# Scattering rows by source: an index bound on the indirect DMAs, or real places for the padding rows

## The chip, the cores and the metric

The kernel runs on one core of one Trainium2 chip. The metric is the device time of one execution in microseconds (us); less is better. Three timed executions of the kernel before gave 6073.62, 6076.83 and 6087.9 us.

## What is computed

A graph of N = 6250 nodes with 128 features and E = 106250 edges (50000 drawn pairs in both directions, and a loop for each node), sorted by destination, goes through four layers, each followed by a layer norm of the sum with its input:

```python
x = _layernorm(x + _L0_gnn_ref(...))   # attention over the edges into each node, 8 heads
x = _layernorm(x + _L1_gnn_ref(...))   # an MLP per edge, summed by destination
x = _layernorm(x + _L2_gnn_ref(...))   # a filter per edge times a projected row, summed by destination
x = _layernorm(x + _L3_gnn_ref(...))   # gated layer
```

The change concerns how the last layer gets its second mean. In `_L3_gnn_ref` both directions of each edge are used:

```python
a_in  = _seg_mean(feat_in[src], dst, N)    # mean over the edges into a node
a_out = _seg_mean(feat_out[dst], src, N)   # mean over the edges out of a node
h = _gru_cell(jnp.concatenate((a_in, a_out), axis=1), h, ...)
```

The first mean follows the order in which the edges lie. The second needs them by source, and they are sorted by destination.

## The kernel before, in words

**Tiles.** Nodes lie in buckets of P = 128 (NB = 49). The edges, sorted by destination, are cut into tiles of 128 so that no tile spans two buckets; a bucket's last tile is padded. There are TILES = 880 tiles, 4 (U) to a batch, 220 (BATCHES) batches, and R = 4 ring slots of one batch each. 880 x 128 = 112640 places stand for 106250 edges, so 6390 rows are padding.

**Stages.** The program is a row of stages in order of time, each with its own loops on all engines and with a barrier behind it: a short set-up, attention (126 to 1345 us of the span), the edge MLP (1451 to 2566), the filter layer (2610 to 3718, and its end), the scatter of rows by source (3738 to 4897) and the gated layer (4907 to 6026, and its end). In four of these GpSimd (POOL) gathers one row for each edge with `gather_rows`: one indirect DMA per tile, four per batch, with no bound on the index. In the fifth it scatters.

**The scatter.** The class `RowsBySource` takes one batch k at a time. SP loads the tile's local destination numbers (`load`, L762), VectorE makes a one-hot of them (`one_hot`, L2081), TensorE multiplies it with the node rows (`rows_of`, L2089), ScalarE puts 128 features, a one and the local source number into a row of REV = 130 words, 520 bytes (`pack`, L2096 and L2098), and POOL sends each tile's 128 rows to their places in the table `by_src` in device memory (`scatter`, L2105). `pack` waits until the scatters that used the same ring slot four batches earlier have landed. The first EARLY = 12 batches are done in the filter layer's block, the other 208 in `stage_rows_by_src`, whose POOL loop ends with a wait for all landings (L2117 is the end of that block).

**The places.** The table has RB = 256 blocks of 512 rows (SLOTS_R = 131072), filled in layer 1 with rows that count for nothing. The place of each row is an integer in `key_i`. It is worked out in the filter layer by VectorE in 16 steps of `number(n)` (L1678 to L1715), one per batch from batch R = 4 on, each on 128x880 values; `numbered` counts them. In step 7 the padding rows get a place beyond the table (`wrong`, 4 x SLOTS), step 11 makes the integers, steps 12 to 15 make the local source numbers. A padding row's index is beyond SLOTS_R - 1, and the bound makes the DMA leave that row out:

```python
pool.indirect_dma_start(self.table, bass.IndirectOffsetOnAxis(place, 0), self.out[:, r, u, :], None,
                        bounds_check=SLOTS_R - 1, oob_is_err=False).then_inc(self.scattered[r], 16)
```

Three engines wait for `numbered` to reach 16 before they start on the early batches: SP ahead of its first twelve `load`s, ScalarE ahead of the first `pack`, VectorE ahead of the memset of the ones (L1874). The gated layer reads the 256 blocks of the table in order (L2252).

Of the kernel before, what the change touches and what calls it, by code (L numbers as in the profile page):

```python
# [21 lines left out]
ALU = mybir.AluOpType  # L22
# [7 lines left out]
P = 128  # L30
# [8 lines left out]
U = 4  # L39
R = 4  # L40
KR, FR = 6, 7
TILES = -(-(E // P + NB) // (U * R)) * U * R
# [3 lines left out]
RB = (E + NB * QUAD) // QUAD  # L46
SLOTS_R = RB * QUAD
# [3 lines left out]
REV = F + 2  # L51
# [95 lines left out]
def arena(c, start, shape, dtype=F32):  # L147
    n = 1
    for s in shape:
        n *= s  # L150
    words = n if dtype != BF16 else n // 2
    ap = c.arena[:, start:start + words]
    if dtype != F32:
        ap = ap.bitcast(dtype)
    if len(shape) == 2:
        return ap.rearrange("p (a b) -> p a b", b=shape[1])
    if len(shape) == 3:
        return ap.rearrange("p (a b c) -> p a b c", b=shape[1], c=shape[2])
    return ap
# [537 lines left out]
def is_first(k):  # L697
    return isinstance(k, int) and k == 0
# [9 lines left out]
def bucket_in_turn(nc, c, n, engine):  # L708

    return nc.values_load_multi_w_load_instructions(  # L710
        c.order[:, n:n + 1], engines=(engine,), min_val=0, max_val=NB - 1,
        skip_runtime_bounds_check_because="the vector engine made them within these bounds")[1][0]
# [586 lines left out]
def stage_edges(nc, c, name, table, acc, buckets, local, layer, h1, next_rows=None):  # L1299
# [5 lines left out]
    with ExitStack() as ctx:  # L1305
# [34 lines left out]
        if layer == 2:  # L1340
            by_tile = arena(c, SPOTS0, [JC, P])
            slot, high7, high9, wrong = (arena(c, RANKS0 + n * TILES, [TILES]) for n in range(4))
            row = arena(c, NUMBERS0, [TILES])
            whole, shifted = (arena(c, NUMBERS0 + n * TILES, [TILES], I32) for n in range(1, 3))
            pslot, spotted, numbered = pb("pslot", [P, 2, 512]), sem("spotted"), sem("numbered")
# [32 lines left out]
        @block.sync  # L1378
        def _(sp):
            def send_row(k):  # L1380
                n = BUCKET_AT.get(k)
                if n is None:
                    return
                at = bucket_in_turn(nc, c, n, SP_ENGINE)
                sp.wait_ge(kept, n + 1)
                sp.dma_start(next_rows[bass.ds(at, 1), :, :].rearrange("one p f -> p (one f)"), keep[:, n % 3, :]).then_inc(row_sent[n % 3], 16)

            def step(k, i, r):
                if layer == 1 and k >= 17:
                    send_row(k - 17)  # L1390
                if k >= BATCHES:
                    return
                e0 = loaded_values(nc, c.edge0, k, SP_ENGINE, E - 1)

                at_least(sp, ready, k - R + 1, tick)
                if layer == 1:
                    at_least(sp, hots_t, k - R + 1, tick)
                    load_local_rows(sp, c, rows, k, r, rows_in)
                for u in range(U):
                    to = attr[u * A1:(u + 1) * A1, r, :] if layer == 1 else attr[:, r, u * P:(u + 1) * P]  # L1400
                    sp.dma_start(to, attr_dram[:, bass.ds(e0[u], P)]).then_inc(attributes[r], 16)
                if layer == 1:
                    if k == R * NB + 8:
                        sp.wait_ge(ranked, 3 + 6 * NB)
                        sp.dma_start(c.slots.rearrange("(p n) -> p n", p=P), slot_of).then_inc(slotted, 16)
                    if is_first(k):
                        sp.wait_ge(start, 3)
                        sp.dma_start(next_rows[NT - 1:NT, :, :].rearrange("one p f -> p (one f)"), filler[:, 0, 0:F]).then_inc(filled, 16)
                    for b in range(k, RB, BATCHES):
                        sp.dma_start(c.by_src[bass.ds(b, 1), :, :, :].rearrange("one p u f -> p (one u) f"), filler[:, :, :]).then_inc(filled, 16)  # L1410
            if layer == 1:
                sp.dma_start(src_i, c.src.rearrange("(p n) -> p n", p=P)).then_inc(sources, 16)
            rounds(sp, BATCHES, R, step)
            if layer == 2:
                sp.wait_ge(numbered, 16)
                for k in range(EARLY):
                    c.by_source.load(sp, k)
            if layer == 1:
                for k in range(BATCHES, BATCHES + 17):
                    step(k, k // R, k % R)  # L1420
                sp.wait_ge(slotted, 16)
                sp.wait_ge(filled, 16 * (RB + 1))
                for n in range(3):
                    sp.wait_ge(row_sent[n], 16 * len(range(n, NB, 3)))

        @block.scalar
        def _(act):
# [91 lines left out]
            def pack_early(k, i, r):  # L1519
                b = k + 14 - BATCHES - EARLY_LAG  # L1520
                if 0 <= b < EARLY:
                    if b == 0:
                        act.wait_ge(numbered, 16)
                        act.wait_ge(c.by_source.start, 1)
                    c.by_source.pack(act, b, pt)

# [125 lines left out]
        def _(dve):  # L1652
# [25 lines left out]
            def number(n):  # L1678
                if n == 0:
                    dve.wait_ge(spotted, 1)  # L1680
                if n:
                    dve.wait_ge(numbered, n)
                if n == 0:
                    ins = dve.tensor_copy(slot[:, 0:512], pslot[:, 0, :])
                if n == 1:
                    ins = dve.tensor_copy(slot[:, 512:TILES], pslot[:, 1, 0:TILES - 512])
                if n == 2:
                    ins = dve.tensor_copy(whole, slot)
                if n == 3:
                    ins = dve.tensor_scalar(shifted, whole, 7, None, ALU.arith_shift_right)  # L1690
                if n == 4:
                    ins = dve.tensor_copy(high7, shifted)
                if n == 5:
                    ins = dve.tensor_scalar(shifted, whole, 9, None, ALU.arith_shift_right)
                if n == 6:
                    ins = dve.tensor_copy(high9, shifted)
                if n == 7:
                    ins = dve.tensor_scalar(wrong, c.key[:, :], 0.0, float(4 * SLOTS), ALU.is_lt, ALU.mult)
                if n == 8:
                    ins = dve.scalar_tensor_tensor(out=row, in0=slot, scalar=4.0, in1=wrong, op0=ALU.mult, op1=ALU.add)  # L1700
                if n == 9:
                    ins = dve.scalar_tensor_tensor(out=row, in0=high7, scalar=-511.0, in1=row, op0=ALU.mult, op1=ALU.add)
                if n == 10:
                    ins = dve.scalar_tensor_tensor(out=row, in0=high9, scalar=508.0, in1=row, op0=ALU.mult, op1=ALU.add)
                if n == 11:
                    ins = dve.tensor_copy(c.key_i, row)
                if n == 12:
                    ins = dve.tensor_scalar(shifted, c.gather_i[:, :], 7, None, ALU.arith_shift_right)
                if n == 13:
                    ins = dve.tensor_copy(high7, shifted)  # L1710
                if n == 14:
                    ins = dve.tensor_copy(high9, c.gather_i[:, :])
                if n == 15:
                    ins = dve.scalar_tensor_tensor(out=c.src_local[:, :], in0=high7, scalar=-float(P), in1=high9, op0=ALU.mult, op1=ALU.add)
                ins.then_inc(numbered, 1)  # L1715

# [124 lines left out]
            def step(k, i, r):  # L1841
# [20 lines left out]
                    cut_off(k - CUT_AT)  # L1862
                if layer == 1 and CUT_AT + 8 <= k < CUT_AT + 10:
                    cut_off(k - CUT_AT - 4)
                if layer == 2 and R <= k < R + 16:
                    number(k - R)
                for lag, part in node_steps:
                    if k - lag in BUCKET_AT:
# [1 line left out]
                b = k - BATCHES - EARLY_LAG  # L1870
                if layer == 2 and 0 <= b < EARLY:
                    if b == 0:
                        dve.wait_ge(numbered, 16)
                        dve.memset(c.by_source.out[:, :, :, F:F + 1], 1.0).then_inc(c.by_source.start, 1)  # L1874
                    c.by_source.one_hot(dve, b)
            rounds(dve, BATCHES, R, step, peeled=2)
            for k in range(BATCHES, BATCHES + 17):
                step(k, k // R, k % R)
# [181 lines left out]
class RowsBySource:  # L2060
# [39 lines left out]
    def scatter(self, pool, k):  # L2100
        r = k % R
        pool.wait_ge(self.packed, 2 * (k + 1))
        for u in range(U):
            place = self.c.key_i[:, k * U + u:k * U + u + 1]
            pool.indirect_dma_start(self.table, bass.IndirectOffsetOnAxis(place, 0), self.out[:, r, u, :], None,  # L2105
                                    bounds_check=SLOTS_R - 1, oob_is_err=False).then_inc(self.scattered[r], 16)

EARLY, EARLY_LAG = 12, 2
# [374 lines left out]
def gnn_kernel(nc, t, out):  # L2484
    c = Core(nc)
    scratch = lambda name, shape: nc.dram_tensor(name, shape, F32, kind="Internal").ap()
    c.by_src = scratch("rows_by_src", (RB, P, U, REV))
    c.slots = scratch("slots", (EP,))
    c.kv3 = scratch("keys_values", (NT, P, 2 * F))
    c.kv = c.kv3.rearrange("t p f -> (t p) f")  # L2490
# [83 lines left out]
```

## Time and profile before

| what | value |
|---|---|
| timed runs, median (lowest to highest) | 6076.83 us (6073.62 to 6087.9) |
| the profiled execution's own time | 6069.62 us |
| its span, first to last instruction | 6067.6 us |
| busy: POOL, TensorE, VectorE, ScalarE | 4297.3, 3856.3, 3649.1, 2834.3 us |
| five sweeps of 880 indirect DMAs on POOL | 838.8 to 869.3 us busy each |
| granted TensorE clock, mean | 0.776 |

The profiled execution's time and its span are 2.0 us apart; what is worked out from its rows is set against its own 6069.62 us. Busy times are sums over the whole span. An engine whose busy share is high in every stage is a candidate for the bound of each; whether it is shows in who waits for whom inside a stage. "Issue" in a list of waits is idle time in which the profile sees nothing that the engine waited for.

### The profile page before, as it was taken

The numbers are of one execution on the slowest core, as the hardware profiler recorded it, in microseconds if no ns is written. First come the engines' busy times: TensorE is split into PE (matmuls) and PEld (weight loads), VectorE is DVE, ScalarE is ACT, GpSimd is POOL, SyncE is SP. The second block draws the span as 40 slices with busy tenths as digits, with TensorE's granted clock in tenths as the row PEclk, the third lists the DMA queues.
The fourth block names the chain that finished last, engine by engine and source line by source line (L and its number), as shares of the span: only waits on it lengthen the run. The fifth ranks groups of instructions, "written<-read, shape, count | busy, mean of one in ns | idle before, by whom it ended". The sixth has DMA issues, their size and how long they took to land. (4 is left out here: it accounts for less than half of the span.)

```text
span 6067.6 us, 93535 instructions
## 1 busy us (share of the span) xinstructions
PE 3856.3 (64%) x20652; PEld 3144.4 (52%) x20652; DVE 3649.1 (60%) x11761; ACT 2834.3 (47%) x6936; POOL 4297.3 (71%) x4477
## 2 busy tenths in 40 slices
PE   5567767765666767678888876344343446666665
PEld 4566666664555555546556554333333346665443
DVE  6788888886988888667777774111001034445665
ACT  3788888882111111355555563111111158884444
POOL 2677777663777777767777776677777777777775
PEclk8787787787999898878888887555555579898777
DMA  4444444453655555622223324332222245553223
GB/s 125 123 134 129 128 129 128 123 117 103 189 148 147 147 148 148 126 64 74 74 74 74 74 74 62 100 77 77 77 75 75 73 115 168 163 164 89 59 59 46
DMA packets 485366, 649.31 MB, mean 107 GB/s; under 512 B 120187, under 2 KB 332938, under 8 KB 484822
## 3 DMA queue, kind: packets, MB, share of 16 engines
q0 software_dynamic: 155552, 345.75, 22.9%
q1 hardware_dynamic: 329271, 297.58, 18.2%
q8 instruction: 187, 3.06, 0.2%
q14 instruction: 356, 2.92, 0.2%
HBM read 495.44 MB, written 150.71 MB: 106 GB/s over the span
## 5 line engine op out<-in xcount | busy, mean ns | idle before, releaser
L694 POOL DMA_INDIRECT kv_ring<-keys_values,gather_i x880 | 860.8, 978 | 363.9 <-issue 247.9
L2105 POOL DMA_INDIRECT rows_by_src<-arena,key x880 | 869.3, 988 | 309.7 <-issue 260.2
L694 POOL DMA_INDIRECT e_ring<-filter_rows,gather_i x880 | 838.8, 953 | 304.8 <-issue 268.0
L694 POOL DMA_INDIRECT e_ring<-table,gather_i x880 | 845.7, 961 | 287.2 <-issue 264.6
L694 POOL DMA_INDIRECT arena<-table,gather_i x880 | 850.6, 967 | 278.8 <-issue 266.7
L2089 PE MATMUL rs_ph<-nodes,arena 128*128 x1664 | 424.4, 436 | 667.7 <-ACT arena L2098 615.6
L2089 PEld LDWEIGHTS rs_ph<-nodes,arena 128*128 128x128 f32 x1664 | 365.5, 324 | 726.9 <-issue 726.9
L2081 DVE TENSOR_SCALAR arena<-arena,part 128x512 f32<-128x512 bf16 x220 | 113.6, 519 | 949.2 <-PE rs_ph L2089 898.3
L1565 PE MATMUL e_pa<-e_msg,e_hot 128*128 128x128 f32 x3520 | 552.5, 308 | 37.0 <-DVE e_msg L1768 30.2
L743 DVE TENSOR_TENSOR arena<-arena,e_pa 128x128 f32 x1760 | 496.9, 282 | 110.8 <-PE e_pa L1565 81.9
L2331 PE MATMUL gl_sum_f<-arena,gl_hot_f 128*128 128x128 f32 x1760 | 292.8, 318 | 425.3 <-DMA arena<-table,gather_i 198.5
L1565 PEld LDWEIGHTS e_pa<-e_msg,e_hot 128*128 128x128 f32 x3520 | 511.5, 223 | 49.2 <-DVE e_msg L1768 41.9
L930 PE MATMUL at_pa<-at_msg,at_hot 128*128 128x145 f32 x1760 | 356.7, 359 | 235.0 <-DVE at_msg L1200 148.6
L2096 ACT ACTIVATE arena<-src_local 128x4 f32<-128x4 bf16 x220 | 45.8, 208 | 972.5 <-DMA rows_by_src<-arena,key 934.5
L2331 PEld LDWEIGHTS gl_sum_f<-arena,gl_hot_f 128*128 128x128 f32 x1760 | 253.1, 221 | 463.7 <-issue 242.8
L1546 PE MATMUL e_ph<-l_w1e_by_tile,e_attr 128*128 128x512 f32 x440 | 274.4, 709 | 334.0 <-DVE e_tmp L1763 313.3
L930 PEld LDWEIGHTS at_pa<-at_msg,at_hot 128*128 128x128 f32 x1760 | 300.2, 239 | 278.7 <-DVE at_msg L1200 214.8
L1445 ACT ACTIVATE e_msg<-e_tmp 128x512 f32<-128x512 f32 x220 | 138.6, 630 | 634.4 <-DVE e_tmp L1763 625.8
L1537 PE MATMUL e_pt<-e_attr,L_mlp_w_held 50*128 50x512 f32 x440 | 279.2, 718 | 172.0 <-DVE e_soft L1774 169.1
L2278 ACT ACTIVATE gl_hot_r<-j,arena 128x128 f32<-128x128 f32 x1024 | 324.4, 387 | 136.1 <-PE gl_sum_r L2322 103.7
L886 PE MATMUL at_pq<-arena,at_hot_t 128*128 x1760 | 325.4, 344 | 54.3 <-ACT at_hot_t L1000 44.3
L1548 PEld LDWEIGHTS e_ph<-arena,e_hot_t 128*128 128x128 f32 x1760 | 276.4, 225 | 126.1 <-issue 126.1
(461 smaller groups left out, 9821.1 us busy)
## 6 DMA issues: line engine op xcount, KB each, us to landing
rows_by_src<-e_filler SPq DMA_DIRECT2D x256, 260.0 KB
arena<-rows_by_src SPq DMA_DIRECT2D x256, 260.0 KB
at_rows<-local_rows SPq DMA_DIRECT2D x220, 128.0 KB
e_rows<-local_rows SPq DMA_DIRECT2D x220, 128.0 KB
arena<-local_rows SPq DMA_DIRECT2D x220, 128.0 KB, 3.3
e_attr<-edge_attr SPq DMA_DIRECT2D x880, 25.0 KB
kv_ring<-keys_values,gather_i POOLq DMA_INDIRECT x880
e_ring<-table,gather_i POOLq DMA_INDIRECT x880
```

Of the source, the lines that this page charges most:

```text
L694: pool.indirect_dma_start(ring[:, r, u, :], None, table, bass.IndirectOffsetOnAxis(index, 0)).then_inc(arrived[r], 16)
L743: self.dve.tensor_tensor(to, to, self.psum[:, u, 0:self.width], ALU.add).then_inc(self.added, 1)
L886: ins = pe.matmul(pq[:, q, u, 0:QW], hot_t[:, q, u, :], c.query[:, bass.ds(which[u], 1), :].rearrange("p one f -> p (one f)"), start=True, ...
L930: ins = pe.matmul(pa[:, u, 0:C_END], hot[:, q, u, :], msg[:, q, u, :], start=True, stop=True)
L1537: pe.matmul(pt[:, r % 2, :, :].rearrange("p u f -> p (u f)"), c.w["mlp_w0"][:, :], attr[:, r, :], start=True, stop=True).then_inc(ready, 1)
L1546: pe.matmul(ph[:, q, :, :].rearrange("p u f -> p (u f)"), attr[:, r, :], c.w["w1e_by_tile"][:, :], start=True, stop=False)
L1548: ins = pe.matmul(ph[:, q, u, :], hot_t[:, r, u, :], c.by_dst[:, bass.ds(which[u], 1), :].rearrange("p one f -> p (one f)"), start=False, ...
L1565: ins = pe.matmul(pa[:, q, u, :], hot[:, r, u, :], msg[:, q, u, :], start=True, stop=True)
L2089: ins = pe.matmul(ph[:, k % 2, u, :], self.hot_t[:, k % R, u, :], self.c.x[:, bass.ds(which[u], 1), :].rearrange("p one f -> p (one f)"), ...
L2105: pool.indirect_dma_start(self.table, bass.IndirectOffsetOnAxis(place, 0), self.out[:, r, u, :], None, bounds_check=SLOTS_R - 1, oob_is_er ...
L2278: act.activation(hot_r[:, r, u, :], c.j[:, 0:P], ACT.Abs, bias=ring_r[:, j % RR, u, F + 1:F + 2], scale=-1.0).then_inc(hots_r, 1)
L2331: ins = pe.matmul(sum_f[:, q, u, :], hot_f[:, r, u, :], ring_f[:, k % FR, u, :], start=True, stop=True)
```

## The change

The scatter loses its bound, and with it the register that holds the bound. The table gets R = 4 more blocks of 512 rows behind its 256, which is 2048 rows or sixteen tiles' worth; they are neither filled nor read. The list of places gets two more steps and another last one: step 11 writes 128 j + p for the sixteen columns j and the partitions p into the first 16 columns of `wrong` (whose values have been used by then), step 12 subtracts SLOTS_R from each place and takes the smaller of that and 128 (tile mod 16) + p, and step 13 adds SLOTS_R again and makes the integers. A real place less SLOTS_R is negative and stays; a padding row's is large and becomes its own row in the added blocks. The old steps 12 to 15 become 14 to 17, and the waits for 16 become waits for 18.

```diff
             if layer == 2:
-                sp.wait_ge(numbered, 16)
+                sp.wait_ge(numbered, 18)
...
                     if b == 0:
-                        act.wait_ge(numbered, 16)
+                        act.wait_ge(numbered, 18)
...
                 if n == 11:
-                    ins = dve.tensor_copy(c.key_i, row)
+                    ins = dve.tensor_scalar(wrong[:, 0:R * U], c.j[:, 0:R * U], float(P), c.part[:, 0:1], ALU.mult, ALU.add)
                 if n == 12:
+                    by_slot = row.rearrange("p (g s) -> p g s", s=R * U)
+                    ins = dve.scalar_tensor_tensor(out=by_slot, in0=by_slot, scalar=-float(SLOTS_R), op0=ALU.add, op1=ALU.min,
+                                                   in1=wrong[:, 0:R * U].unsqueeze(1).broadcast_to([P, TILES // (R * U), R * U]))
+                if n == 13:
+                    ins = dve.tensor_scalar(c.key_i, row, float(SLOTS_R), None, ALU.add)
+                if n == 14:
                     ins = dve.tensor_scalar(shifted, c.gather_i[:, :], 7, None, ALU.arith_shift_right)
...
-                if layer == 2 and R <= k < R + 16:
+                if layer == 2 and R <= k < R + 18:
                     number(k - R)
...
                     if b == 0:
-                        dve.wait_ge(numbered, 16)
+                        dve.wait_ge(numbered, 18)
...
-            pool.indirect_dma_start(self.table, bass.IndirectOffsetOnAxis(place, 0), self.out[:, r, u, :], None,
-                                    bounds_check=SLOTS_R - 1, oob_is_err=False).then_inc(self.scattered[r], 16)
+            pool.indirect_dma_start(self.table, bass.IndirectOffsetOnAxis(place, 0), self.out[:, r, u, :], None)\
+                .then_inc(self.scattered[r], 16)
...
-    c.by_src = scratch("rows_by_src", (RB, P, U, REV))
+    c.by_src = scratch("rows_by_src", (RB + R, P, U, REV))
```

## Rows read from the trace of the kernel before

**Rows 1.** The page, busy time, share of the span and instructions of each engine.
```profile
PE 3856.3 (64%) x20652; PEld 3144.4 (52%) x20652; DVE 3649.1 (60%) x11761; ACT 2834.3 (47%) x6936; POOL 4297.3 (71%) x4477
```
**Rows 2.** The page's costliest groups: line, engine, operation, count | busy us, mean ns | idle.
```profile
L694 POOL DMA_INDIRECT kv_ring<-keys_values,gather_i x880 | 860.8, 978 | 363.9 <-issue 247.9
L2105 POOL DMA_INDIRECT rows_by_src<-arena,key x880 | 869.3, 988 | 309.7 <-issue 260.2
L694 POOL DMA_INDIRECT e_ring<-filter_rows,gather_i x880 | 838.8, 953 | 304.8 <-issue 268.0
...
L694 POOL DMA_INDIRECT arena<-table,gather_i x880 | 850.6, 967 | 278.8 <-issue 266.7
```
**Rows 3.** Timeline of POOL amid the scatter: start us, busy us, what [idle before].
```profile
4199.32 0.98 POOL L2105 DMA_INDIRECT rows_by_src<-arena,key  x1 [0.30 <-issue]
...
4210.91 0.98 POOL L2105 DMA_INDIRECT rows_by_src<-arena,key  x1 [0.30 <-issue]
```
**Rows 4.** Timeline of POOL amid the filter layer's gather, the same columns.
```profile
2612.08 0.94 POOL L694 DMA_INDIRECT e_ring<-filter_rows,gather_i  x1 [0.30 <-issue]
...
2624.56 0.94 POOL L694 DMA_INDIRECT e_ring<-filter_rows,gather_i  x1 [0.30 <-issue]
```
**Rows 5.** Line L2105: duration ns minimum/median/maximum, first and last start us.
```profile
L2105 POOLq MOVE  x880: 29/29/38, 3738.1 to 4879.8; - x176
L2105 POOL DMA_INDIRECT rows_by_src<-arena,key x880: 977/982/1937, 3738.9 to 4895.5; - x176
...
DMA to landing us min/median/max: 2.1/2.4/6.9
```
**Rows 6.** Line L694, two of its four gathers, the same columns.
```profile
L694 POOL DMA_INDIRECT kv_ring<-keys_values,gather_i x880: 940/946/1857, 126.4 to 1343.2; - x176
...
L694 POOL DMA_INDIRECT e_ring<-filter_rows,gather_i x880: 940/944/1905, 2610.8 to 3716.6; - x176
```
**Rows 7.** Waits from 3738 to 4897: us in total, times, longest us.
```profile
ACT arena L2096 <- DMA rows_by_src<-arena,key: 934.5, 210, 7.3
...
POOL rows_by_src L2105 <- ACT arena L2098: 28.0, 23, 21.3
POOL rows_by_src L2105 <- ACT arena L2096: 21.5, 3, 20.9
```
**Rows 8.** Line L2117, the end of the scatter's block: ns, start us.
```profile
L2117 ACTq DRAIN  x1: 721/721/721, 4877.1 to 4877.1; - x1
...
L2117 POOLq DRAIN  x1: 8536/8536/8536, 4897.9 to 4897.9; - x1
```
**Rows 9.** Lines L1375 and L403, gathers of rows of 4 and 12 bytes.
```profile
L1375 POOL DMA_INDIRECT arena<-slots,cols_i x7: 941/944/947, 2565.6 to 2573.1; - x7
DMA to landing us min/median/max: 10.8/12.5/15.3
...
L403 POOL DMA_INDIRECT arena<-edges,cols_i x7: 942/946/2261, 109.3 to 118.4; - x7
```
**Rows 10.** DMA from 4878 to 4900: queue, packets, MB, share; issues, us to landing.
```profile
q0 software_dynamic: 480, 0.01, 1.6%
...
rows_by_src<-arena,key POOLq DMA_INDIRECT x15, 2.1
```
**Rows 11.** DMA from 3900 to 4850, the same columns.
```profile
q0 software_dynamic: 23600, 47.78, 14.7%
...
rows_by_src<-arena,key POOLq DMA_INDIRECT x738, 2.5
```
**Rows 12.** VectorE's groups by form from 2630 to 2760: steps 9 and 11.
```profile
L1702 DVE SCALAR_TENSOR_TENSOR arena<-arena 128x880 f32<-128x880 f32 x1 | 1.1, 1070 | 0.0
...
L1706 DVE CAST key<-arena 128x880 int32<-128x880 f32 x1 | 0.6, 615 | 0.0
```
**Rows 13.** Waits in the filter layer (POOL 2610 to 3718, VectorE 2630 to 3700).
```profile
POOL e_ring L694 <- issue: 268.0, 879, 0.3
...
DVE e_msg L1768 <- DMA e_ring<-filter_rows,gather_i: 148.1, 138, 3.0
```

More of the change, by code:

```diff
@@ L1705, in number @@
                 if n == 11:
-                    ins = dve.tensor_copy(c.key_i, row)
+                    ins = dve.tensor_scalar(wrong[:, 0:R * U], c.j[:, 0:R * U], float(P), c.part[:, 0:1], ALU.mult, ALU.add)
                 if n == 12:
+                    by_slot = row.rearrange("p (g s) -> p g s", s=R * U)
[4 more added lines that the diff above has]
+                if n == 14:
                     ins = dve.tensor_scalar(shifted, c.gather_i[:, :], 7, None, ALU.arith_shift_right)
-                if n == 13:
+                if n == 15:
                     ins = dve.tensor_copy(high7, shifted)
-                if n == 14:
+                if n == 16:
                     ins = dve.tensor_copy(high9, c.gather_i[:, :])
-                if n == 15:
+                if n == 17:
                     ins = dve.scalar_tensor_tensor(out=c.src_local[:, :], in0=high7, scalar=-float(P), in1=high9, op0=ALU.mult, op1=ALU.add)
```

## The prediction

> **What bounds the kernel now.** I read the page's busy shares first. GpSimd (POOL) is the busiest engine with 4297.3 us, 71% of a span of 6067.6 us [rows 1]; VectorE and TensorE stay near 60%. The costliest groups say what POOL does: five sweeps of 880 indirect DMAs, one per tile of 128 rows, four gathers and one scatter by source. Each sweep keeps POOL for 839 to 869 us and adds about 0.3 us of idle time per DMA that the trace calls "issue" [rows 2]. So POOL paces five stages one after another, and what an indirect DMA costs on POOL is multiplied by 880.
>
> Then I compared the shape of one DMA. The timeline of POOL in the middle of the scatter has starts at 4199.32 and, nine DMAs later, at 4210.91 [rows 3]: 11.59 / 9 = 1.288 us each, of which 0.98 is busy and 0.30 idle. In the middle of a gather, ten DMAs take from 2612.08 to 2624.56 [rows 4]: 1.248 us each, 0.94 busy and again 0.30 idle. The views of the two lines say the same: the scatter takes 977/982/1937 ns (minimum, median, maximum) [rows 5], the gathers 940/944 or 946 [rows 6]. The scatter is 38 ns longer in its median and 37 in its minimum, and its idle time is the same.
>
> The reader should see a third thing: nobody else holds the scatter stage back. ScalarE (ACT) waits 934.5 us for scatters to land, 210 times, while POOL waits for ACT next to nothing: 28.0 us at L2098, of which 21.3 are the one wait before the first scatter, and 21.5 us at L2096, of which 20.9 are the one wait where the next block starts [rows 7]. At the end every other engine has long drained: ACT at 4877.1, POOL starts its own drain at 4897.9, takes 8.5 us, and only then does the last stage begin [rows 8]. What POOL saves in this stage therefore moves the end of the program.
>
> **What the change takes away: the bound.** Of the 880 scatters each loses its bound and one register move. The move (29 ns, on POOL's queue) runs ahead of the DMAs: the last move is at 4879.8, the last scatter at 4895.5 [rows 5], and the gathers have the same 0.30 us gap without a move [rows 3, 4]. I price it at nothing; were it in the path, it would give 880 x 0.029 = 25.5 us.
>
> The bound itself has no row without its scatter, so it is bounded from two sides. Upper end: all that parts scatter from gather is the bound, 880 x (1.288 - 1.248) = 35.2 us by the pitches, 880 x 38 ns = 33.4 us by the medians. Lower end, no gain: the 38 ns belong to the direction or to the row of 520 bytes, and stay. A middle value comes from the sums instead of the medians: 869.3 - 850.6 = 18.7 us against the last gather and 869.3 - 838.8 = 30.5 us against that of layer 2, with 869.3 - 860.8 = 8.5 us against the attention's as the lowest [rows 2]; but the gathers' sums hold more long outliers, since their stages run beside a busier VectorE, and the scatter keeps its own few. I take 33.4 us, for this reason: the gathers differ among themselves in everything but the bound and cost the same. Rows of 1024 bytes cost 946 and rows of 512 bytes 944 [rows 6], rows of 4 bytes from the slots 944, rows of 12 bytes of the edge list 946 [rows 9]. Twelve is no power of two either, so 520 is unlikely to be what costs. That leaves direction or bound, and I hold the bound the likelier: the minimum moves with the median, as a fixed extra step would do it.
>
> On direction a page bears. No row here parts the two.
>
> **What it adds: rows that are written.** The edge list has 106250 edges in 880 x 128 = 112640 places, so 6390 rows that were dropped are now written, 6390 x 520 B = 3.3 MB. Per DMA on POOL this costs nothing: the last 15 scatters move 0.01 MB between them [rows 10], so they are padding through and through, and they have the same 0.98 us as the full ones (all 880 lie at a median of 982, [rows 5]). The scatters of the middle move 47.78 MB in 738 DMAs, 64.7 KB each, at 14.7% of the DMA engines' time [rows 11]: 3.3 MB more is a fourteenth on top, beside POOL. In path is only the last DMA's landing, now empty with 2.1 us [rows 10], then full like the middle ones with 2.5 [rows 11]: +0.4 us. Sixteen tiles of separate places are as many as the four ring slots of four tiles can have in flight, so a place is only written again after its earlier DMA has landed.
>
> **What it adds: two steps of VectorE in layer 2.** The list of places takes 18 steps instead of 16, one per batch. The new wide one is a SCALAR_TENSOR_TENSOR on 128x880; its like takes 1.07 us (L1702). The one on 16 columns costs no more than a whole-width step, 0.6 us, and the last replaces a CAST of 0.6 us by a TENSOR_SCALAR of the same size [rows 12]. Together at most 1.7 us of VectorE, in two of 220 batches. POOL hides them: in that whole stage it never waited for VectorE, only for "issue" (879 times 0.3 us), while VectorE waited 148.1 us for gathered rows [rows 13]. With no cover they would cost 1.7 us. The two steps before them push the four steps for the source numbers two batches back. The waits for 16 become waits for 18: on SP the first twelve loads of rows stand behind it, on ACT the packing, on VectorE the first one-hot; step 18 runs in batch 21, and these waits come after batch 219, so they are met long before. The larger table in memory (one MB) is not filled and not read.
>
> **Sum.** 33.4 - 0.4 = 33.0 us less, against the profiled execution's 6069.62 us: 6036.6. Of the 33.4, 48 x 38 ns = 1.8 us lie in the early scatters ahead of the block boundary; POOL is the last there as I read the 20.9 us wait behind it [rows 7], else 1.8 us are lost. The three timed runs have a median of 6076.83, 7.2 above the profiled one, and spread from 6073.6 to 6087.9; on that median the forecast is 6043.8, which I give.
>
> **Rivals.**
> - *The bound is free and the 38 ns are the direction's.* For it: no unbounded scatter stands in the trace. Against it: gathers of four row sizes with one price. It gives 6076.83 + 0.4, about 6077. Chance 0.22. The Trainium skill's sentence on descriptor generation would point here.
> - *The bound is only a part*, 10 to 20 us by the middle value above: about 6062. Chance 0.06.
> - *The move counts too*: 33 + 25.5 = 58.5 us less, 6018. The equal gaps speak against it. Chance 0.03.
> - *Slower: landing becomes the bound.* ACT may pack a slot only when its scatter of four batches ago has landed. Four batches at the new pitch are 20.0 us; one batch's own issue 5.0 and packing about 0.9 (two ACT steps) leave 14.1 us for the landing, which is now 2.4 and at most 6.9 [rows 5]. If the padding writes, 6390 rows to 2048 places, pushed it above 14.1, each of the 55 turns of the ring would be longer by the excess: from 14.7 us on the saving is gone, and at 16 us it is 55 x 1.9 = 104.5 us more, less 33, about 6148. A landing of 12.5 us does stand in the trace, for the slots' gather [rows 9], still under the limit, and the scatters take only 14.7% of the DMA engines' time [rows 11]. Chance 0.03.
>
> **How the numbers follow.** The forecast case (saving 18.7 to 35.2 us) has 0.66 and its own range, with some 6 us of spread from run to run, 6035 to 6060. To leave out no more than two in ten the range must reach the free bound at 6077 as well: 6034 to 6080. About 0.3% (18 us) is what a measurement can tell from no change here: faster 0.66 + 0.03 = 0.69, same 0.22 + 0.06 = 0.28, slower 0.03.
>
> **What would show each step.** Right: scatters with a median of 940 to 946 ns, the gap still 0.30, pitch 1.25; a stage from first to last scatter of some 1123 us instead of 1157; the last 15 scatters moving about 1 MB; ACT's wait for landings shorter by about the same 33 us; gathers unchanged. Wrong: a median of 982 (direction), anything between (part), a gap of 0.27 (the move), POOL waiting for ACT L2096 many times (landing), or POOL waiting for VectorE around batch 20 of layer 2. The prediction falls as a whole if the unbounded scatter's duration is not that of the gathers.

## The result and the profile after

| | time, median | to the kernel before |
|---|---|---|
| before, 14 runs | 6081.50 us (6073.62 to 6087.90) | |
| changed, 14 runs | 6070.53 us (6065.81 to 6076.07) | 0.9981 [0.9974, 0.9989] |

The change saves 11 us, 0.19%. It is real, since the interval leaves out 1, but it is a third of the 33 us that were forecast and less than the 0.3% that the text counted as a change.

The line of the scatter in the changed kernel, to be held against [rows 5] (the columns are minimum/median/maximum in ns, first and last start in us):

```profile
L2111 POOL DMA_INDIRECT rows_by_src<-arena,key x880: 963/969/1698, 3751.2 to 4896.7; - x176
...
DMA to landing us min/median/max: 2.3/2.4/6.8
```

The median time that one scatter keeps POOL busy has gone from 982 to 969 ns, not to 944. The register move has gone with the bound, and 880 x 13 ns = 11.4 us, which is as much as the 11 us of the gain (by its interval 7 to 16 us). The timeline of POOL amid the scatter shows it against [rows 3]:

```profile
4200.25 0.97 POOL L2111 DMA_INDIRECT rows_by_src<-arena,key  x1 [0.30 <-issue]
4201.53 0.97 POOL L2111 DMA_INDIRECT rows_by_src<-arena,key  x1 [0.31 <-issue]
4202.80 0.97 POOL L2111 DMA_INDIRECT rows_by_src<-arena,key  x1 [0.30 <-issue]
```

The busy part is shorter; the 0.30 us of idle time ahead of each DMA is what it was, though no move stands there any more.

The gathers have not moved. From the view of L694, against [rows 6]:

```profile
L694 POOL DMA_INDIRECT kv_ring<-keys_values,gather_i x880: 940/946/1863, 126.3 to 1347.8; - x176
L694 POOL DMA_INDIRECT e_ring<-table,gather_i x880: 940/944/1627, 1457.1 to 2570.2; - x176
L694 POOL DMA_INDIRECT e_ring<-filter_rows,gather_i x880: 938/944/1931, 2622.2 to 3729.5; - x176
L694 POOL DMA_INDIRECT arena<-table,gather_i x880: 940/944/1467, 4908.7 to 6031.8; - x176
```

Nor has the end of the scatter's block changed, from the view of its line, against [rows 8] (DRAIN is the last instruction but the barrier's that each engine runs in a block):

```profile
L2123 ACTq DRAIN  x1: 721/721/721, 4878.7 to 4878.7; - x1
...
L2123 POOLq DRAIN  x1: 8536/8536/8536, 4899.2 to 4899.2; - x1
```

Here the reader can see why one profiled execution must not be set against another as a whole. This one took 6076.07 us, 6.5 more than the profiled one of before (6069.62), though the kernel is faster. The first scatter starts at 3751.2 instead of 3738.9, so 12.3 us were lost ahead of it. Of these, 11.4 were lost before the first gather of the filter layer (2622.2 instead of 2610.8 [rows 6]), in stages that the change doesn't touch. From the first scatter's start to the last one's it is 4896.7 - 3751.2 = 1145.5 us instead of 4895.5 - 3738.9 = 1156.6 [rows 5], 11.1 less. The last gather sweep then takes 1123.1 us from first to last start instead of 1117.6 (4907.4 to 6025.0 before) and loses 5.5 more: 12.3 - 11.1 + 5.5 = 6.7, the difference of the two executions within 0.2. The stage shows the change; such drifts of other stages are what 14 runs average out.

The waits of the scatter stage in the changed kernel, against [rows 7]: ScalarE's wait for landings is 14.8 us shorter, and POOL still has one long wait for ScalarE at the start and one at the next block.

```profile
ACT arena L2102 <- DMA rows_by_src<-arena,key: 919.7, 209, 6.9
...
POOL rows_by_src L2111 <- ACT arena L2104: 20.8, 1, 20.8
POOL rows_by_src L2111 <- ACT arena L2102: 20.7, 2, 20.4
```

### The profile page after: what moved, and what is told of

Same layout as the page of the kernel before. It is cut to its first block and busy times, and to the rows that moved or that the text cites. A ratio compares the mean times of both kernels' runs of the same rounds, so it can differ in the third digit from the quotient of the medians.

```text
span 6074.2 us, 92657 instructions
## 1 busy us (share of the span) xinstructions
PE 3852.2 (63%) x20652; PEld 3146.3 (52%) x20652; DVE 3649.3 (60%) x11763; ACT 2834.1 (47%) x6936; POOL 4290.5 (71%) x4477
## 5 line engine op out<-in xcount | busy, mean ns | idle before, releaser
L694 POOL DMA_INDIRECT kv_ring<-keys_values,gather_i x880 | 857.2, 974 | 372.1 <-issue 246.7
L2111 POOL DMA_INDIRECT rows_by_src<-arena,key x880 | 858.5, 976 | 308.7 <-issue 267.0
L694 POOL DMA_INDIRECT e_ring<-filter_rows,gather_i x880 | 840.3, 955 | 310.0 <-issue 267.6
L694 POOL DMA_INDIRECT arena<-table,gather_i x880 | 856.1, 973 | 278.9 <-issue 266.7
L694 POOL DMA_INDIRECT e_ring<-table,gather_i x880 | 846.1, 961 | 287.1 <-issue 265.5
```

Source lines behind the costliest of these rows:

```text
L694: pool.indirect_dma_start(ring[:, r, u, :], None, table, bass.IndirectOffsetOnAxis(index, 0)).then_inc(arrived[r], 16)
```

## The experiments

All edits are to the changed kernel, whose scatter reads

```python
pool.indirect_dma_start(self.table, bass.IndirectOffsetOnAxis(place, 0), self.out[:, r, u, :], None)
```

Two questions were open: is it the bound that costs the 13 ns, and whose are the 25 ns that still part the scatter (969) from the gathers (944)? Each run's time is given as a ratio to the kernel before, timed beside it. The reading rests on the medians of one DMA, which repeat to the nanosecond: the untouched scatter of the two runs with a bound on the gathers has 969 again, and the untouched gathers of eight other runs 944 and 946.

**The bound put back, all rows written.**

```diff
-            pool.indirect_dma_start(self.table, bass.IndirectOffsetOnAxis(place, 0), self.out[:, r, u, :], None)\
-                .then_inc(self.scattered[r], 16)
+            pool.indirect_dma_start(self.table, bass.IndirectOffsetOnAxis(place, 0), self.out[:, r, u, :], None,
+                                    bounds_check=SLOTS_R + R * QUAD - 1, oob_is_err=False).then_inc(self.scattered[r], 16)
```

> The changed kernel with a bound put back on the 880 scatters, set behind the added blocks, so that all 112640 rows are written as in the changed kernel and the bound leaves nothing out. Theory A, the bound itself costs POOL 13 ns each time, whatever it drops: median 982 ns as before the change, against 969 without a bound, and some 880 x 13 ns = 11 us more than the changed kernel, the time of the kernel before. Rival, what cost 13 ns was the leaving out of rows: median 969, the time of the changed kernel.

```profile
L2111 POOLq MOVE  x880: 29/29/38, 3755.1 to 4898.3; - x176
L2111 POOL DMA_INDIRECT rows_by_src<-arena,key x880: 977/982/2465, 3756.0 to 4914.0; - x176
```

The median is 982 again, to the nanosecond, and the time is that of the kernel before: 1.0003 [0.9994, 1.0012], an interval that does not touch the changed kernel's. Theory A holds. The run says more: this kernel has everything that the change adds, the 3.3 MB of padding rows, the two steps of VectorE and the waits for 18, and still stands level with the kernel before. What the change adds costs less than can be measured here (the interval is some 5 us to each side); what it gains is the bound.

**The row cut to 512 bytes.**

```diff
+        self.short = c.by_src.rearrange("b p u f -> (b p u f)").rearrange("(n f) -> n f", f=F)
-            pool.indirect_dma_start(self.table, bass.IndirectOffsetOnAxis(place, 0), self.out[:, r, u, :], None)\
+            pool.indirect_dma_start(self.short, bass.IndirectOffsetOnAxis(place, 0), self.out[:, r, u, 0:F], None)\
```

> The changed kernel with each scatter sending the first 512 of the 520 bytes of a row, into the same memory seen as rows of 512 bytes. What it leaves out: the one and the source number of each row, so the second mean of the last layer is not computed; the amount of work is the same. The unbounded scatter took 969 ns where the gathers took 944. Theory B, the 25 ns are the direction's: median still 969, no change in time against the changed kernel. Rival C, they are those of a row of 520 bytes, no power of two: median 944, 880 x 25 ns = 22 us less.

```profile
L2112 POOL DMA_INDIRECT rows_by_src<-arena,key x880: 965/969/1691, 3750.7 to 4893.7; - x176
```

The median is 969: the size of the row is not what parts scatter from gather. The time is 0.9976 [0.9966, 0.9986] of the kernel before, which the changed kernel's interval overlaps.

**The scatter turned into a gather of 520 bytes.** The padding rows are sent to real rows of the table here, the last four blocks of 512, so that nothing is read that was never written.

```diff
-                    ins = dve.scalar_tensor_tensor(out=by_slot, in0=by_slot, scalar=-float(SLOTS_R), op0=ALU.add, op1=ALU.min,
+                    ins = dve.scalar_tensor_tensor(out=by_slot, in0=by_slot, scalar=-float(SLOTS_R - R * QUAD), op0=ALU.add, op1=ALU.min,
-                    ins = dve.tensor_scalar(c.key_i, row, float(SLOTS_R), None, ALU.add)
+                    ins = dve.tensor_scalar(c.key_i, row, float(SLOTS_R - R * QUAD), None, ALU.add)
-            pool.indirect_dma_start(self.table, bass.IndirectOffsetOnAxis(place, 0), self.out[:, r, u, :], None)\
+            pool.indirect_dma_start(self.out[:, r, u, :], None, self.table, bass.IndirectOffsetOnAxis(place, 0))\
-    c.by_src = scratch("rows_by_src", (RB + R, P, U, REV))
+    c.by_src = scratch("rows_by_src", (RB, P, U, REV))
```

> The changed kernel with the scatter turned about: 880 unbounded gathers of rows of 520 bytes from the same table, with nearly the same indices, into the same ring. What it leaves out: nothing is written to the table, so the second mean is not computed. Theory B, direction: median 944 as the other gathers, 22 us less than the changed kernel. Rival C, row of 520 bytes: median 969, the time of the changed kernel. Both in part: between.

```profile
L2111 POOL DMA_INDIRECT arena<-rows_by_src,key x880: 940/944/2023, 3753.8 to 4876.7; - x176
```

Same place in the program, same ring, nearly the same list of places (the padding rows' are others), same row of 520 bytes, other direction: 944. Theory B holds. The time is 0.9936 [0.9921, 0.9951] of the kernel before, 30 to 48 us less; the 13 and 25 ns give 33. From first to last start the stage takes 4876.7 - 3753.8 = 1122.9 us, 33.7 less than before the change: that is the saving and the stage (some 1123 us) that the prediction had for 38 ns.

**A bound on the gathers.**

```diff
-            pool.indirect_dma_start(ring[:, r, u, :], None, table, bass.IndirectOffsetOnAxis(index, 0)).then_inc(arrived[r], 16)
+            pool.indirect_dma_start(ring[:, r, u, :], None, table, bass.IndirectOffsetOnAxis(index, 0),
+                                    bounds_check=N - 1, oob_is_err=False).then_inc(arrived[r], 16)
```

> The changed kernel with a bound on all 3520 gathers of the four other sweeps, which no index exceeds. Theory A, a bound costs 13 ns on every indirect DMA: medians 957 instead of 944 (959 instead of 946 in the attention), 3520 x 13 ns = 46 us more than the changed kernel, less what the attention's sweep hides since it waits for ScalarE at times: 6105 to 6116. Rival, the bound costs only in a scatter: medians 944, time of the changed kernel.

```profile
L694 POOL DMA_INDIRECT kv_ring<-keys_values,gather_i x880: 992/998/1842, 126.5 to 1345.3; - x176
L694 POOL DMA_INDIRECT e_ring<-table,gather_i x880: 992/997/1271, 1455.3 to 2612.6; - x176
L694 POOL DMA_INDIRECT e_ring<-filter_rows,gather_i x880: 992/997/2167, 2666.1 to 3818.2; - x176
L694 POOL DMA_INDIRECT arena<-table,gather_i x880: 992/997/1508, 4999.6 to 6169.7; - x176
```

Neither expectation held. A bound costs a gather 53 ns, four times what it costs the scatter, and the kernel's time is 1.0202 [1.0186, 1.0217] of before. Against the changed kernel that is 1.0202 / 0.9981, 2.2%, some 134 us; three sweeps of 880 x 53 ns are 140. From first to last start these three are 44.2, 44.8 and 47.0 us longer than in the changed kernel, 136 together. The fourth, the attention's, gives almost nothing: it runs from 126.5 to 1345.3, 1218.8 us. In the ten profiled kernels without a bound on the gathers it takes 1216.8 to 1228.3. Its row among the groups (busy us, mean ns | idle us before it and what ended it) says where the cost went; compare the first row of [rows 2]:

```profile
L694 POOL DMA_INDIRECT kv_ring<-keys_values,gather_i x880 | 898.1, 1021 | 329.2 <-issue 256.9 <-ACT arena L1016 38.0 <-DVE at_prod L1132 26.7
```

POOL is busy 37.3 us longer and idle 34.7 us less: in that sweep ScalarE and VectorE hold POOL back, and a dearer gather only fills the waits.

**The same bound from a register that is loaded once.** Since the gather pays 53 ns, the move of 29 ns ahead of each DMA became suspect again.

```diff
+    bound = pool.alloc_register(f"bound_of_gathers{len(c.used)}_{batches[0]}")
+    pool.reg_mov(bound, N - 1)
-            pool.indirect_dma_start(ring[:, r, u, :], None, table, bass.IndirectOffsetOnAxis(index, 0)).then_inc(arrived[r], 16)
+            pool.indirect_dma_start(ring[:, r, u, :], None, table, bass.IndirectOffsetOnAxis(index, 0),
+                                    bounds_check=bound, oob_is_err=False).then_inc(arrived[r], 16)
```

> The changed kernel with the bound on all 3520 gathers again, but the bound is put into a register once per sweep instead of by a 29 ns move before each DMA. With the moves the gathers took 997 ns against 944 without a bound, and the kernel 2.0% more than the one before. Theory A, the 53 ns are the work on the indices: median still 997, time still 2.0% above the kernel before. Rival, the move is in the path: 997 - 29 = 968, some 3 x 880 x 29 ns = 77 us less than with the moves, 0.8% above the kernel before.

```profile
L696 POOL DMA_INDIRECT kv_ring<-keys_values,gather_i x880: 992/998/1850, 127.3 to 1355.2; - x176
L696 POOL DMA_INDIRECT e_ring<-table,gather_i x880: 992/997/1263, 1468.4 to 2622.8; - x176
```

No row of moves stands in this profile; the median is 997 again and the time 1.0206 [1.0189, 1.0223] of before. The move costs nothing that shows, as the prediction read from the equal gaps. The attention's sweep takes 1227.9 us here, inside the same spread as above.

**Half the rows, both directions, with and without a bound.** These runs, with one execution each, ask whether the prices are per row or per instruction. Four of them send 64 rows. In all five the padding rows have real places in the last four blocks, by the same edit as in the run that turned the scatter into a gather, and where there is a bound it is `SLOTS_R - 1`, which no index exceeds. Two send the first 64 rows of each scatter:

```diff
-            place = self.c.key_i[:, k * U + u:k * U + u + 1]
-            pool.indirect_dma_start(self.table, bass.IndirectOffsetOnAxis(place, 0), self.out[:, r, u, :], None)\
+            place = self.c.key_i[0:64, k * U + u:k * U + u + 1]
+            pool.indirect_dma_start(self.table, bass.IndirectOffsetOnAxis(place, 0), self.out[0:64, r, u, :], None)\
```

> The changed kernel with each unbounded scatter sending only the first 64 of its 128 rows. What it leaves out: half of the rows by source, so the second mean is wrong in its terms. With 128 rows: 969 ns, the gathers 944. Theory D, POOL pays per instruction and hardly per row: median above 940. Rival, it pays per row: near half, 485 ns. Either way it is the base for the run with a bound beside it.

> The kernel with 64 rows per scatter and a bound put back, which no index exceeds. With 128 rows the bound cost 13 ns. If the bound is a test of each index: 6 to 7 ns above the run without it. If it is a fixed step per instruction: 13 ns above it.

The other two gather 64 rows in its place. Between them stands a gather of 128 rows with a bound, to see whether the 53 ns hold here too:

> The run with the scatter turned into a gather of 520-byte rows, with 64 instead of 128 rows in each of the 880. What it leaves out: the table by source is not written, so the second mean is not computed. The scatter went from 969 to 897 ns when its rows were halved, 72 ns for 64 rows. If the 25 ns between scatter and gather are paid per row, the gather with 64 rows lies 12 to 13 ns below the scatter with 64, at 884. If they are a fixed step of the direction: 25 ns below, at 872.

> The same gather of 520-byte rows in the scatter's place, 128 rows, with a bound that no index exceeds. What it leaves out: as before, nothing is written to the table. Unbounded it took 944 ns. If the bound's price depends on the direction, as the four other sweeps say (53 ns on a gather, 13 ns on a scatter), the median is 997. If it depends on the place in the program or on the row, and 13 ns is what this place pays: 957.

> The gather of 64 rows of 520 bytes in the scatter's place, with a bound that no index exceeds. What it leaves out: the table by source is not written. Unbounded, 64 rows took 899 ns; with 128 rows a bound took a gather from 944 to 997, 53 ns. If a gather's bound is paid per index: 26 to 27 ns more, 926. If it is a fixed step: 952. On the scatter it was per index (13 ns for 128 rows, 7 for 64), so 926 is the likelier.

The rows of L2111 in the five kernels, in the order of the expectations:

```profile
L2111 POOL DMA_INDIRECT rows_by_src<-arena,key x880: 892/897/1894, 3752.9 to 4832.6; - x176
```
```profile
L2111 POOL DMA_INDIRECT rows_by_src<-arena,key x880: 900/904/1840, 3749.0 to 4839.0; - x176
```
```profile
L2111 POOL DMA_INDIRECT arena<-rows_by_src,key x880: 893/899/2027, 3746.8 to 4831.3; - x176
```
```profile
L2111 POOL DMA_INDIRECT arena<-rows_by_src,key x880: 991/997/1811, 3744.3 to 4913.7; - x176
```
```profile
L2111 POOL DMA_INDIRECT arena<-rows_by_src,key x880: 932/937/1688, 3745.3 to 4862.5; - x176
```

All medians of this one place together, in ns:

| | 64 rows | 128 rows | more for 64 rows |
|---|---|---|---|
| scatter, no bound | 897 | 969 | 72 |
| scatter, bound | 904 | 982 | 78 |
| gather, no bound | 899 | 944 | 45 |
| gather, bound | 937 | 997 | 60 |

Halving the rows took the scatter to 897 ns: neither the median above 940 of Theory D nor the 485 of its rival, though far nearer to a price per instruction. On a scatter the bound costs 7 ns for 64 rows and 13 for 128, in line with a price per index, as one of the two expectations had it. On a gather of 128 rows it costs 53 ns in this place too (997), so its price goes by the direction and not by the place or the row. With 64 rows it is 38 ns (937 instead of the 926 or 952 expected), which is neither half (26) nor the same, so a fixed part and one per row. The 25 ns of the direction were expected at 12 or at 25 with half the rows and are not there at all: 897 against 899. The scatter pays more per row (72 ns for 64 rows against 45) and has less of a fixed part. With two sizes only, the straight line between them is an assumption; what makes the scatter's rows dearer stays open.

The profile's page calls durations on POOL rough, so the reader should hold them against the starts. From first to last start the stage is 66.6 us shorter than before the change with 64 rows and a bound, and 76.9 without; for the gathers it is 72.1 (64 rows) and 39.4 (64 rows, bound) shorter and 12.8 longer (128 rows, bound). The medians times 880 give 68.6, 74.8, 73.0, 39.6 and 13.2. The kernels' times, in the order of the expectations, are 6010.73, 6012.14, 6002.05, 6098.25 and 6028.16 us, with the kernel before at 6091.87, 6091.87, 6086.69, 6086.69 and 6092.48 beside them. Single executions are too few for a reading to the microsecond.

One more thing got shorter with 64 rows, in both directions and with or without a bound: POOL's drain at the end of this block. It is 1676 ns in all four runs, and 8536 or 8541 ns in all eight with 128 rows. No run says why.

```profile
L2123 POOLq DRAIN  x1: 1676/1676/1676, 4835.1 to 4835.1; - x1
```

## Why the prediction was wrong, point by point

- **What bounds the stage: right.** Each of the runs moved by 880 times what the DMA's median moved wherever POOL paces the sweep: 13 ns gave 11 us, and where the run with the gather of 520 bytes took all 38 ns away, the stage gave 33.7.
- **The term of the bound: the step that failed.** The text took 33.4 us on the ground that gathers of four row sizes cost the same, so that size could be ruled out, and then held the bound likelier than the direction. Ruling out the size was right (969 with 512 bytes as with 520). But of the two that were left nothing in the trace parted one from the other, and the truth was both: the bound 13 ns, 11.4 us, and the direction 25 ns, 22 us. A minimum that moves with the median speaks for any fixed extra, the direction's as well as the bound's; it was no argument. The rival in which the bound is only a part held with 10 to 20 us, and was given 0.06; its size came from sums of busy time that the text itself called disturbed by outliers, so that it came out right owes something to luck. The measured 6070.53 us lies within 6034 to 6080 only because that range was stretched to take in a free bound; the forecast case's own 6035 to 6060 is missed. (From the text's figures, a saving of 18.7 us and a spread of 6, its upper end would be 6064.)
- **The pages.** The reading of the Trainium skill's GPSIMD Engine Reference, section 4 (a pair of cores, one for each side's descriptors), as a reason for scatter and gather to cost alike is not borne out: at 128 rows they are 25 ns apart, at 64 rows level. That they cost alike was the text's inference; the page gives the pair of cores, and no run here shows them. The Trainium skill's DMA: Bandwidth & Descriptors page, on the anatomy of one DMA, calls descriptor generation small. Here 64 more rows cost 45 to 78 ns, and a bound on 128 indices 13 to 53, which is small against one DMA. It is not free, as the text had inferred: it came to 0.2% of the kernel for 880 scatters and 2.2% for 3520 gathers.
- **The move: right.** 997 ns with a move before each gather and without.
- **The padding rows: right.** The last 16 scatters of the changed kernel now carry 1.07 MB, where the last 15 carried 0.01 before [rows 10], at 0.97 us each like the full ones:

```profile
q0 software_dynamic: 530, 1.07, 14.9%
...
rows_by_src<-arena,key POOLq DMA_INDIRECT x16, 2.3
```

  Their landing is 0.2 us later than before, where the sum had 0.4, and even that is not in the path: the drain that ends the block is 8536 ns in both, and the next gather starts 12.0 us after the last scatter instead of 11.9. The 3.3 MB are nearer to a seventeenth than to the text's fourteenth of what all 880 scatters move (112640 x 520 B = 58.6 MB); nothing hangs on it.
- **The two steps of VectorE: right.** In the filter layer the new wide step took 1065 ns (forecast 1070), the one that replaces the cast 612, and the one on 16 columns (L1706) 232, less than the 0.6 us allowed for it:

```profile
L1709 DVE SCALAR_TENSOR_TENSOR arena<-arena 128x880 f32<-128x880 f32 x1 | 1.1, 1065 | 0.0
...
L1712 DVE TENSOR_SCALAR key<-arena 128x880 int32<-128x880 f32 x1 | 0.6, 612 | 0.0
```

  POOL's waits for VectorE in that stage are one of 0.3 us, and the run with the bound put back stands level with the kernel before.
- **The other rivals.** Landing stayed at 2.4 us in the median and 6.8 at most, far from 14.1.
- **The base.** The three runs of before that the forecast stood on had a median of 6076.83; over 14 runs it is 6081.50. The forecast time was off by this 4.7 as well, but the error is the 22 us of the term.

No run tried a version that does the same work in less. The direction can't simply be turned, since the edges by source are made by this scatter, and the bound is gone already. What the runs with 64 rows suggest, and nobody tried, is fewer DMAs with more rows each: 64 rows more cost 45 to 78 ns, and a DMA of 64 rows with its gap costs 1.2 us.

## What to carry to other kernels

Before a difference between two instructions is put down to one of their properties, count the properties in which they differ; where two are left and no row varies one alone, the forecast is a split between them, not the whole to the likelier. A bound on an indirect DMA is paid on POOL whether or not it drops a row, so where POOL paces a sweep it pays to give the out-of-range indices a real row and to leave the bound out, much more so on gathers (53 ns on 1.25 us) than on scatters (13 of 1.29). Where another engine paces the sweep, as in the attention here, even 53 ns on each of 880 DMAs did not show above the spread of that stage.

## What the runs showed of the hardware that was not expected

- A bound costs a gather of 128 rows 53 ns and a scatter 13; with 64 rows 38 and 7.
- An unbounded scatter of 128 rows keeps POOL busy 25 ns longer than a gather does; with 64 rows the two are within 2 ns.
- Halving the rows of an indirect DMA takes only 45 to 78 ns off some 950. The 0.30 us between two of them are the same with 64 rows as with 128. Nor does the time on POOL depend on the bytes of a row: gathers of rows of 4 to 1024 bytes take 944 to 946 ns [rows 6, 9], scatters of 512 and 520 bytes 969.
- Rows that the bound drops save POOL nothing: the median is 982 ns with 6390 rows left out and 982 with all written, and the last 15 scatters before the change, all padding [rows 10], keep POOL 0.98 us each like the others.
- The drain of POOL that ends the block took 8.5 us behind DMAs of 128 rows and 1.7 behind DMAs of 64.
